# Local attention: probabilities turned by a product with a diagonal, with new step orders and a new share of PSUM evacuations

## What is computed

```python
def attn_layer(x, Wqkv, qs, ksc, Wo):          # b = 32, n = 128, 16 heads of 64
    q, k, v = split(x @ Wqkv)                  # x: tokens shifted by one in half of the channels
    q = l2norm(q) * qs
    k = l2norm(k) * ksc
    q = q * cos * scale + rotate_half(q) * sin * scale
    k = k * cos / scale + rotate_half(k) * sin / scale
    return local_attention(q, k, v) @ Wo       # then + x

sim = einsum('bhwie,bhwje->bhwij', bq, bk2) * 8
sim = where(mask, -max, sim)                   # a key must be 0 to 32 tokens back
out = einsum('bhwij,bhwje->bhwie', softmax(sim, -1), bv2)
```

## Time and profile before

| | us |
|---|---|
| median of 3 runs | 4737.64 (4727.8 to 4738.17) |
| the profiled execution | 4730.3 |
| its span, first to last instruction | 4728.5 |
| busy TensorE (products) | 4209.7 (89%) |
| busy TensorE (weight loads, beside the products) | 2771.7 (59%) |
| busy VectorE | 3747.4 (79%) |
| busy ScalarE | 3498.7 (74%) |
| busy GpSimd | 3211.7 (68%) |
| mean granted TensorE clock | 0.939 of full speed |

### The profile page before, as it was taken

How to read it: one execution, slowest core, us unless ns; L and a number is a source line. 1 busy time by engine, 2 the same in 40 slices (tenths; PEclk the granted TensorE clock), 3 DMA queues, 4 the chain that set the end, 5 groups by cost and what they waited for, 6 DMA issues and landing times. The chain is left out here.

```text
span 4728.5 us, 153694 instructions
## 1 busy us (share of the span) xinstructions
PE 4209.7 (89%) x50950; PEld 2771.7 (59%) x50950; DVE 3747.4 (79%) x8958; ACT 3498.7 (74%) x12854; POOL 3211.7 (68%) x4351
## 2 busy tenths in 40 slices
PE   6949899997999989998899988999889998777775
PEld 3426556664666646666466664666646666455543
DVE  4769889983999749997499965999569995688398
ACT  6938788883899838897389874899658895588335
POOL 2422289982999839997399964999559995344162
PEclk8969999998999989999999998999999999788886
DMA  2000000000000000000000000000000000000000
GB/s 60 0 20 1 5 2 0 0 1 25 2 0 0 1 25 2 0 0 19 6 2 0 0 19 6 2 0 0 19 7 1 0 0 20 2 0 0 13 15 19
DMA packets 36173, 34.82 MB, mean 7 GB/s; under 512 B 11303, under 2 KB 31013, under 8 KB 34853
## 3 DMA queue, kind: packets, MB, share of 16 engines
q1 hardware_dynamic: 35876, 31.13, 2.3%
HBM read 29.03 MB, written 2.10 MB: 7 GB/s over the span
## 5 line engine op out<-in xcount | busy, mean ns | idle before, releaser
L2227 ACT ACTIVATE local_prob<-ps,local_shift_by 128x128 f32<-128x128 f32 x3072 | 1078.5, 377 | 10.0 <-DVE local_shift_by L2307 9.8
L2155 POOL TENSOR_TENSOR local_qk<-local_qk,local_rsin 128x512 f32<-128x512 f32 x768 | 968.2, 1271 | 58.8 <-DVE local_rsin L2332 58.7
L2162 POOL TENSOR_TENSOR local_qk<-local_qk,local_inv 128x512 f32<-128x512 f32 x768 | 792.7, 1044 | 127.1 <-ACT local_inv L2246 126.4
L2466 PE MATMUL ps<-local_wqkv,local_xsT 128*128 128x512 f32 x1536 | 830.9, 627 | 50.0 <-DVE local_rsin L2332 24.9
L2169 POOL TENSOR_TENSOR local_prob<-local_prob,local_rs 128x512 f32<-128x512 f32 x768 | 790.8, 1042 | 12.6 <-DVE local_rs L2314 12.6
L2227 ACT ACTIVATION_READ_ACCUMULATOR local_prob<-ps,local_shift_by 128x1 f32 x3072 | 670.6, 218 | 0.0
L2321 DVE TENSOR_TENSOR local_qk<-ps,local_cos_t 128x512 f32<-128x512 f32 x768 | 525.4, 684 | 92.3 <-ACT local_sq L2235 90.2
L2307 DVE TENSOR_REDUCE local_shift_by<-ps 128x4 f32<-128x512 f32 x768 | 524.5, 683 | 84.7 <-PE ps L2542 84.7
L2332 DVE TENSOR_TENSOR local_rsin<-ps,local_sin_t 128x256 f32<-128x256 f32 x1536 | 572.0, 414 | 0.0
L2235 ACT ACTIVATE local_sq<-ps 128x512 f32<-128x512 f32 x768 | 466.8, 608 | 101.4 <-PE ps L2466 86.1
L2339 DVE TENSOR_REDUCE local_ss<-local_sq 128x8 f32<-128x512 f32 x768 | 513.0, 669 | 6.0 <-ACT local_sq L2235 6.0
(11 more groups left out here) (334 smaller groups left out, 8654.3 us busy)
## 6 DMA issues: line engine op xcount, KB each, us to landing
local_wqkv<-L_ffn_Wqkv SPq DMA_DIRECT2D x7, 1536.0 KB, 6.5
local_wo<-L_ffn_Wo SPq DMA_DIRECT2D x7, 512.0 KB, 7.3
out<-quantised_res SPq DMA_DIRECT2D x8, 256.0 KB, 2.3
local_w<-L_ffn_W SPq DMA_DIRECT2D x6, 341.0 KB
L_cross_decay<-c_decay SPq DMA_DIRECT2D x1, 1024.0 KB, 11.8
local_w<-L_ffn_W SPq DMA_DIRECT2D x12, 64.0 KB
load_raw<-L_ffn_w SPq DMA_DIRECT2D x8, 64.0 KB, 2.1
local_b<-L_ffn_b SPq DMA_DIRECT2D x24, 0.5 KB
```

What stands on the lines that cost most here:

```text
L2155: nc.gpsimd.tensor_tensor(qk[w][:, j, :, :], qk[w][:, j, :, :], rsin[j % 2][:, :, :], ALU.add).then_inc(rot_ready, 1)
L2162: nc.gpsimd.tensor_tensor(qk[w][:, j, :, :], qk[w][:, j, :, :], bcast(inv[:, w, 8 * j:8 * j + 8].unsqueeze(2), [P, 8, LH]), ALU.mult).then ...
L2227: last = nc.scalar.activation(prob[w][:, g, j, :], ps[:, 4 + g % 2, j * P:(j + 1) * P], ACT.Exp, bias=shift_by[:, w, h:h + 1], accum_out=s ...
L2466: nc.tensor.matmul(proj_bank(j), xsT[w][:, :], wqkv[:, 512 * j:512 * j + 512], start=True, stop=True).then_inc(proj_ready, 1)
```

## The change

- A new constant `ident2`, two 64x64 identities above each other, loaded at the start.
- A new tile `diag` of 64 columns a head. `normalise` no longer touches `prob`; it writes `diag` = `ident2` times the reciprocals, 128x256 for a group of 4 heads.
- `turn_probs` computes the product of `prob` with `diag` (f32) in place of the transpose of `prob`.
- `evacuate_values` and `evacuate_heads` are all on ScalarE. Of the four `evacuate_qk` of a block ScalarE keeps one (half 1, p 0) and VectorE makes three.
- All four engines have a new order of the same functions. The waits for PSUM banks in `project`, `project_values`, `turn_qk` and `turn_probs` have new numbers that follow from it.

```diff
+    diag = [sb(f"diag{u}", [P, G, HG, LH]) for u in range(2)]
...
             def normalise(b, w, g, live):
                 if live(b):
                     pool.wait_ge(rsum_ready, 4 * b + g + 1)
-                    nc.gpsimd.tensor_tensor(prob[w][:, g, :, :], prob[w][:, g, :, :],
-                                            bcast(rs[:, w, HG * g:HG * g + HG].unsqueeze(2), [P, HG, P]),
+                    nc.gpsimd.tensor_tensor(diag[w][:, g, :, :], bcast(env["ident2"][:, :].unsqueeze(1), [P, HG, LH]),
+                                            bcast(rs[:, w, HG * g:HG * g + HG].unsqueeze(2), [P, HG, LH]),
                                             ALU.mult).then_inc(prob_ready[g], 1)
...
-                                last = nc.tensor.transpose(ps[:, 2 + p, (4 * i + j) * LH:(4 * i + j) * LH + LH],
-                                                           prob[w][r, 2 * half + i, j, :], ident[r, r])
+                                last = nc.tensor.matmul(ps[:, 2 + p, (4 * i + j) * LH:(4 * i + j) * LH + LH],
+                                                        prob[w][r, 2 * half + i, j, :], diag[w][r, 2 * half + i, j, :],
+                                                        start=True, stop=True)
...
-            def evacuate_values(b, w, half, live):
...
-            def evacuate_heads(b, w, half, live):
...
+    c["c_ident2"] = np.concatenate([np.eye(LH, dtype=f)] * 2, 0)
```

The new orders (ScalarE, the steps around the probabilities; TensorE, the whole turn):

```diff
             def step(n, u, live):
                 v = 1 - u
-                evacuate_heads(n + 1, v, 0, live)
                 evacuate_x(n + 5, v, live)
+                evacuate_probs(n + 2, u, 0, 1, live)
+                evacuate_probs(n + 2, u, 0, 0, live)
+                squares(n + 4, u, 1, live)
+                exponentials(n + 2, u, 2, live)
+                evacuate_values(n + 3, v, 1, live)
+                exponentials(n + 2, u, 3, live)
...
+                evacuate_heads(n + 2, u, 0, live)
+                squares(n + 4, u, 3, live)
+                evacuate_probs(n + 2, u, 1, 1, live)
+                evacuate_probs(n + 2, u, 1, 0, live)
+                exponentials(n + 3, v, 0, live)
+                exponentials(n + 3, v, 1, live)
                 evacuate_qk(n + 3, v, 1, 0, live)
+                evacuate_values(n + 4, u, 0, live)
...
-                turn_qk(n - 2, u, 0, live)
-                output(n - 5, v, live)
-                project(n - 1, v, 3, live)
-                turn_x(n, u, live)
-                turn_probs(n - 4, u, 1, live)
-                weighted_values(n - 4, u, 0, live)
-                scores(n - 2, u, 0, live)
-                turn_qk(n - 2, u, 1, live)
-                project_values(n - 2, u, 0, live)
-                project(n, u, 0, live)
-                shift(n - 5, v, live)
-                project(n, u, 1, live)
-                weighted_values(n - 4, u, 1, live)
-                turn_probs(n - 3, v, 0, live)
-                project_values(n - 2, u, 1, live)
-                project(n, u, 2, live)
-                scores(n - 2, u, 1, live)
-            sequence_loop(pe, NB, 0, 5, step)
+                turn_x(n + 5, v, live)
+                turn_qk(n + 2, u, 1, live)
+                weighted_values(n + 1, v, 1, live)
+                scores(n + 2, u, 1, live)
+                turn_probs(n + 2, u, 0, live)
+                project(n + 4, u, 1, live)
+                project_values(n + 3, v, 1, live)
+                shift(n, u, live)
+                weighted_values(n + 2, u, 0, live)
+                turn_qk(n + 3, v, 0, live)
+                project(n + 4, u, 2, live)
+                project(n + 4, u, 3, live)
+                scores(n + 3, v, 0, live)
+                turn_probs(n + 2, u, 1, live)
+                output(n + 1, v, live)
+                project_values(n + 4, u, 0, live)
+                project(n + 5, v, 0, live)
+            sequence_loop(pe, NB, 5, 0, step)
```

More of the change, by code:

```diff
@@ L2174, in step @@
                 v = 1 - u
[L2175 to L2191, removed]
+                copy_for_values(n + 4, u, live)
+                to_unit(n + 2, u, 3, live)
+                rotate(n + 3, v, 2, live)
+                rotate(n + 3, v, 3, live)
+                normalise(n + 2, u, 0, live)
+                fetch(n + 6, u, live)
+                normalise(n + 2, u, 1, live)
+                to_unit(n + 3, v, 2, live)
+                to_unit(n + 3, v, 0, live)
+                to_unit(n + 3, v, 1, live)
+                rotate(n + 4, u, 0, live)
+                keep(n, u, live)
+                normalise(n + 2, u, 2, live)
+                low_half(n, u, live)
+                normalise(n + 2, u, 3, live)
+                rotate(n + 4, u, 1, live)
+            sequence_loop(pool, NB, 6, 0, step)
         @block.scalar
@@ L2274, in step @@
                 v = 1 - u
-                evacuate_heads(n + 1, v, 0, live)
                 evacuate_x(n + 5, v, live)
+                evacuate_probs(n + 2, u, 0, 1, live)
[4 more added lines that the diff above has]
+                exponentials(n + 2, u, 3, live)
+                high_half(n, u, live)
+                squares(n + 4, u, 2, live)
+                log_variance(n - 1, v, live)
+                over_deviation(n - 1, v, live)
+                evacuate_heads(n + 2, u, 0, live)
[4 more added lines that the diff above has]
+                exponentials(n + 3, v, 1, live)
                 evacuate_qk(n + 3, v, 1, 0, live)
-                exponentials(n + 3, v, 0, live)
+                evacuate_values(n + 4, u, 0, live)
                 squares(n + 5, v, 0, live)
                 log_norms(n + 4, u, live)
-                high_half(n, u, live)
+                evacuate_heads(n + 2, u, 1, live)
                 over_norms(n + 4, u, live)
[L2283 to L2296, removed]
             sequence_loop(act, NB, 5, 1, step)
@@ L2402, in step @@
[L2402 to L2420, removed]
+                aggregate(n - 5, v, live)
+                one_over_sums(n - 2, u, 1, live)
+                norm(n - 6, u, live)
+                bound_norms(n - 1, v, live)
@@ new lines, in step @@
+                cosines(n, u, 0, live)
+                sines(n, u, 0, live)
+                maxima(n - 2, u, 2, live)
+                maxima(n - 2, u, 3, live)
+                cosines(n, u, 1, live)
+                sines(n, u, 1, live)
+                sums_of_squares(n, u, 0, live)
+                one_over_sums(n - 2, u, 2, live)
+                evacuate_qk(n - 1, v, 0, 0, live)
+                evacuate_qk(n - 1, v, 0, 1, live)
+                one_over_sums(n - 2, u, 3, live)
+                sums_of_squares(n, u, 1, live)
@@ new lines, in step @@
+                cosines(n, u, 2, live)
+                sines(n, u, 2, live)
+                maxima(n - 1, v, 0, live)
+                cosines(n, u, 3, live)
+                sines(n, u, 3, live)
+                maxima(n - 1, v, 1, live)
+                statistics(n - 4, u, live)
+                residual(n - 3, v, live)
+                sums_of_squares(n, u, 2, live)
+                sums_of_squares(n, u, 3, live)
+                one_over_sums(n - 1, v, 0, live)
+                evacuate_qk(n - 1, v, 1, 1, live)
@@ L2422, in _ @@
+            sequence_loop(dve, NB, 0, 6, step)
         @block.tensor
@@ L2448, in project @@
                         if isinstance(b, int):
-                            wait(pe, vals_ready[1], b - 2)
+                            wait(pe, vals_ready[1], b - 1)
                             wait(pe, rot_step, 4 * b - 3)
                     elif j == 1:
-                        wait(pe, vals_ready[0], b - 1)
+                        wait(pe, vals_ready[0], b)
                         if isinstance(b, int):
@@ L2458, in project @@
                         if isinstance(b, int):
-                            wait(pe, vals_ready[0], b - 1)
+                            wait(pe, vals_ready[0], b)
                             wait(pe, rot_step, 4 * b - 1)
                     else:
-                        wait(pe, vals_ready[1], b - 1)
+                        wait(pe, vals_ready[1], b)
                         if isinstance(b, int):
@@ L2472, in project_values @@
                     if half == 0:
[L2473 removed]
+                        wait(pe, rot_step, 4 * b + 3)
                         if isinstance(b, int):
[L2475 removed]
+                            wait(pe, rot_step, 4 * b + 2)
                             wait(pe, vals_ready[0], b)
                     else:
[L2478 removed]
+                        wait(pe, rot_step, upto(4 * b + 5, 4 * NB))
                         if isinstance(b, int):
[L2480 removed]
+                            wait(pe, rot_step, 4 * b + 4)
                             wait(pe, vals_ready[1], b)
@@ L2868, in residual_layers @@
                "X": sb("X", [P, NB * P]), "XN": sb("XN", [P, NB * P]), "Y": sb("Y", [P, NB * P])}
-        for name, shape in (("ident", [P, P]), ("shift", [P, P]), ("head_rows", [P, HG]),
```

(1 more changed line is left out.)

41 lines of the change are left out of this document (12 added, 29 removed).

## The result

The changed kernel takes 5182.6 us (median of 4, 5171.7 to 5188.8) against 4736.0 us (median of 4), a ratio of 1.094 with a 95% interval of 1.092 to 1.097. The forecast was 5210 us in a range of 5115 to 5330. The profiled execution took 5171.7 us and spans 5169.9 us; before it was 4730.3 and 4728.5.

What follows compares the result with a forecast made beforehand. TensorE was taken to bound local attention. 384 turn_probs steps x 1.28 = +492 us, less 18 absorbed by holes, gave +474 on 4730.3 = 5204; 7 us to the median made 5211, rounded to 5210 us, range 5115 to 5330.

Steps and rivals of the forecast that it cites:

- The bound: Local attention: TensorE, busy 359.8 of 360 us, sets the turn of 14.46 us; the other engines wait for it.
- The product: turn_probs: 16 slots of 0.111 us, set by weight loads, replace 8 of 0.062; +1.28 us a step, 384 steps, +492 us.
- sum of +474 us: Whole kernel: +492 us of longer turn_probs steps, less 18 us absorbed by holes on TensorE.
- 18 absorbed at the ends of the layers: TensorE's idle holes at first probabilities and last turns absorb 3 us in each of 6 layers.
- Orders and share: All engines' new step orders and ScalarE/VectorE's shifted copies: worth 0; tile shape changes bounded at +-58 us.
- GpSimd's saving: normalise at 128x256 saves GpSimd 1.6 us a turn, worth nothing while TensorE sets the turn; upper bound 307 us.
- rival (a): ScalarE's chain, turn_probs half 0 to exponentials 3 to scores half 0, takes over the turn: +96 us, 5305 us; 10%.
- (b): turn_probs: the product is cheap, its load hiding as in the transposes: +174 us, 4910 us; 4%.
- (e): turn_probs: the compiler keeps a transpose-like single pass and the new order neither helps nor hurts: 4738 us; 1%.
- (d): GpSimd really sets the period; its 1.6 us go, ScalarE at 13.7 is next: 146 us gained, 4590 us; 3%.

Runs made afterwards that it cites:

- e2: The kernel before with only the f32 product and the 128x256 diagonal, old orders and share of copies: 5207.5 us, ratio 1.100.
- e7: The kernel before, old orders, with GpSimd's full 128x512 scaling kept and an f32 product with a plain identity in place of the transpose: 5210.0 us.
- e9: The kernel before, old orders and shares, with the product and the diagonal in bf16: 4662.7 us, ratio 0.985.
- e4: The changed kernel with half of each product's moving side left out (32 of 64 diagonal columns): 5182.6 us, one execution.
- e5: The changed kernel with half of each product's stationary side left out (64 of 128 columns of probabilities): 4757.8 us, one execution.
- e8: The changed kernel with transposes of unscaled probabilities in place of the product; GpSimd still writes the 128x256 diagonal, unread: 4679.8 us, ratio 0.989.

## Why the prediction was right

**The bound.** That TensorE alone sets the turn held in the old order without a remainder for the f32 product (e2, e7), and in the new one with 0.03 us to spare before turn_probs half 0. It held for these lengths of step: with the bf16 product in the old order it was 0.17 us a turn short (e9).

**The product.** The step was forecast at 1.92 us and is 1.93; a slot at 0.111 and is 0.111. Both rows behind it carried: that the load and not the product sets the slot (e4 against e5), and that loads of the two 64-row halves run in pairs. The sum of +474 us met +472 in the old order, and both of its terms were near: 492 us of steps and 18 absorbed at the ends of the layers, where the runs have 495 and 23. The product alone explains the slowdown.

The rule of the Trainium skill against this change ("Perfetto Trace Analysis", section "Transposes": turn with transposes, not with standard products) gave the sign, and for f32 this case agrees, at 9.4%. The factor of 4 in "TensorE: Matmul & The Clock Gate", section "Terms" of the Trainium skill, gave 1.98 us as an estimate for a step's slots. Here they are 16 x 0.111 = 1.78 against 8 x 0.062 = 0.50, a factor of 3.6, and the whole step is 1.93 against 0.64 us, 3.0: the rows of loads told more than the factor. For bf16 the rule was not tried: the bf16 product (0.34 us) undercuts the f32 transpose (0.64), and no run has a bf16 transpose.

**Orders and share, taken at 0 with +-58.** They are worth -25 us here, nearly all of what the forecast of 5210 is off (5183). The forecast gave them no sign; that its error is so small is the product's term being right, and a value of 0 that happened to lie near. The steps of a turn, in the mean from 700 to 1000 us, show it as small differences of neighbours: project, project_values and shift sum to 5.71 us where they were 5.81 (e2: 5.80), the two scores to 1.89 where they were 1.94 (e2: 1.93). I counted 11 changes of tile shape in both orders and was right in the count. How much of the 0.14 us a turn each neighbour is worth stays open, and so does what the share is worth without the orders: no run has one without the other.

**GpSimd's saving, taken at 0.** Right for the old order, and for the changed kernel wrong in its reason. It isn't that GpSimd's work hides under TensorE with room to spare; the new order uses the shorter scaling, and without it the change would have cost 58 us more. I looked for such a chain and took another one (rival (a): exponentials 3 to scores half 0, with 0.3 us of room; no hole appeared there, and the room is 0.6: in the turn that starts with turn_probs half 0 at 1375.12 the exponentials end at 1382.10 and scores half 0 start at 1382.71). The chain with no room runs from turn_qk half 1 over VectorE's copy, the reciprocals of group 1 and GpSimd to turn_probs half 0. The prediction followed only ScalarE's list; this chain goes through VectorE's, across the border of its step.

**The rest.** normalise was estimated at 0.63 us and is 0.62. ScalarE at 13.7 us a turn: 289.8 x 16.90 / 360 = 13.6. VectorE at 13.1: 13.4. GpSimd at 12.2: 12.3. Rivals (b) to (e) had their marks at slots of 0.06 or 0.167 or a turn at or under 14.46, and none was seen. e8 speaks against (d) by itself: with GpSimd's lighter work beside TensorE's old work the turn is 14.37 us, not 13.7. The terms of the forecast's range make 5125 to 5300, and 5305 with (a); the ends given, 5115 and 5330, are wider than that, and the prediction doesn't say why.

## What to carry to other kernels

Before moving work onto TensorE, count what it issues there: f32 products come twice, each with its own load, and a product with few moving columns costs its load; in bf16 the same idea paid. When an engine is full, work taken from the others is worth nothing by throughput, but it can still be what the order leans on: test the parts in all combinations before dropping one. The chain to look for in a fixed order leaves the full engine and comes back to it, and a link of it can be a piece of work that has nothing to do with the data and only stands ahead in another engine's list (here a copy of q and k ahead of the reciprocals). So follow every engine's list, across the border of its step too. The room is read from the end of the releaser to the start of the waiting step in two timelines.

## What the runs showed of the hardware

A bf16 load of 128 columns on 64 rows took 0.028 us from pair to pair ((0.29 - 0.095) / 7, one load being 95 ns), the f32 transpose's 0.062, the f32 product's 0.111, twice. I had not expected the bf16 product to be half the price of an f32 transpose.

The exponentials' mean duration rises from 377 to 393 ns in the new order, though the work is the same. Within a run of eight, their starts stay 0.34 us apart while the durations shown climb, here in the changed kernel:

```profile
702.86 0.37 ACT L2228 ACTIVATE local_prob<-ps,local_shift_by 128x128 f32<-128x128 f32 x1
...
705.26 0.42 ACT L2228 ACTIVATE local_prob<-ps,local_shift_by 128x128 f32<-128x128 f32 x1
```

2.40 us for seven steps is 0.343 each. So a mean of the durations shown is not the cost here; that is read from start to start. Why the durations climb stays open.
